# Two preln attention layers with a routed expert layer: fills rearranged, k's rotation and parts on VectorE, experts' tensors at other addresses

## What is computed

```python
x = x + attention0(layernorm(x))   # 16 heads of 16, rotary q and k, window of 128
x = x + experts(layernorm(x))      # 8 experts, the best 2 for each token, silu(a) * b
x = x + attention1(layernorm(x))   # 16 heads of 16, xpos q and k, causal, biases
x = x + ternary(x)                 # x @ quantised weight

# attention1
q_mat = split_heads(x @ Wq.T + bq)
k_mat = split_heads(x @ Wv.T + bv)
v_mat = split_heads(x @ Wk.T + bk)
q_mat, k_mat = _xpos_rotate(q_mat, k_mat)
scores = jnp.einsum('bhqd,bhkd->bhqk', q_mat, k_mat) / math.sqrt(DH * NUM_HEADS)
...
return inter @ Wo.T + bo
```

## Time and profile before

| what | us |
|---|---|
| median of three runs | 2888.07 |
| the three runs | 2873.35, 2892.66, 2888.07 |
| the profiled execution | 2870.61 |
| its span, first to last instruction | 2868.7 |
| TensorE busy | 2463.0 |
| VectorE busy | 1714.3 |
| ScalarE busy | 1350.0 |
| GpSimd busy | 923.1 |

### The profile page before, as it was taken

One profiled execution on the slowest core, in us unless ns is written; L12 is line 12 of the kernel. 1 busy time (PEld: TensorE's weight loads), 2 busy tenths in 40 slices (PEclk: granted clock), 3 DMA queues, 4 the chain that ended last, 5 costly groups with the idle time before them and its releaser, 6 DMA issues. The chain is left out here.

```text
span 2868.7 us, 50929 instructions
## 1 busy us (share of the span) xinstructions
PE 2463.0 (86%) x17722; PEld 1682.5 (59%) x17722; DVE 1714.3 (60%) x5759; ACT 1350.0 (47%) x2419; POOL 923.1 (32%) x863
## 2 busy tenths in 40 slices
PE   3788888888889849999999982799999999998997
PEld 2455555555555528898998872455555555555553
DVE  3666676766667535444444434667676677666651
ACT  2455555555555423333333321255655555555654
POOL 2434555444553220000000015344443434444300
PEclk7899999999999969999999996799999999999998
DMA  4456555666545267877777745444455444444320
GB/s 134 152 185 212 185 181 183 205 213 190 176 156 170 75 205 250 285 267 263 267 280 265 252 146 173 119 119 143 127 146 145 134 119 118 124 135 141 117 62 15
DMA packets 259617, 490.19 MB, mean 171 GB/s; under 512 B 25609, under 2 KB 191113, under 8 KB 249417
## 3 DMA queue, kind: packets, MB, share of 16 engines
q1 hardware_dynamic: 241944, 435.23, 48.3%
q0 software_dynamic: 17456, 52.19, 5.4%
HBM read 299.65 MB, written 186.52 MB: 169 GB/s over the span
## 5 line engine op out<-in xcount | busy, mean ns | idle before, releaser
L672 ACT ACTIVATE a_pr<-a_bank 128x512 f32<-128x512 f32 (+1 forms) x1152 | 638.2, 573 | 571.2 <-PE a_bank L1080 500.6
L941 DVE CUSTOM_DVE_ANT_0 a_junk<-a_bank,a_smask 128x256 bf16<-128x256 f32 (+3 forms) x1536 | 652.1, 463 | 375.2 <-PE a_bank L1177 358.1
L1177 PE MATMUL a_bank<-a_kst,a_qst 96*128 96x256 bf16 (+3 forms) x1536 | 354.5, 297 | 76.5 <-DVE a_nmax L941 26.6
L1203 PE MATMUL a_bank<-a_qst,a_kst 98*128 98x256 bf16 (+3 forms) x1536 | 345.0, 292 | 43.0 <-ACT a_pr L672 25.2
L1221 PE MATMUL a_bank<-a_pr,a_va 128*32 128x256 f32 (+3 forms) x4096 | 350.7, 418 | 28.1 <-ACT a_pr L672 25.3
L1080 PE MATMUL a_bank<-a_mask,a_identb 128*128 128x512 bf16 (+2 forms) x1152 | 351.5, 305 | 0.0
L1177 PEld LDWEIGHTS a_bank<-a_kst,a_qst 96*128 96x128 bf16 x1536 | 127.5, 99 | 268.7 <-issue 84.1
L1426 POOL DMA_DIRECT2D results_dram<-e_yt x39 | 29.3, 751 | 619.2 <-DVE e_yt L1494 601.6
L1449 ACT ACTIVATE e_sa<-e_bank,e_b 128x512 f32<-128x512 f32 (+1 forms) x156 | 101.5, 651 | 255.9 <-PE e_bank L1539 236.0
L550 POOL DMA_INDIRECT xs<-e_rn,e_row x128 | 127.1, 993 | 294.8 <-DMA a_kst<-a_parts_dram 89.0
L1203 PEld LDWEIGHTS a_bank<-a_qst,a_kst 98*128 98x128 bf16 x1536 | 134.0, 99 | 143.7 <-ACT a_pr L672 72.9
(11 more groups left out here) (214 smaller groups left out, 5352.9 us busy)
## 6 DMA issues: line engine op xcount, KB each, us to landing
a_parts_dram<-a_parts SPq DMA_DIRECT2D x224, 256.0 KB
e_under<-ws_dram SPq DMA_DIRECT2D x20, 2048.0 KB, 9.0
e_w<-ws_dram SPq DMA_DIRECT2D x19, 2048.0 KB, 9.2
a_qst<-a_parts_dram SPq DMA_DIRECT2D x96, 384.0 KB, 7.6
a_kst<-a_parts_dram SPq DMA_DIRECT2D x96, 384.0 KB, 8.7
a_parts_dram<-a_parts SPq DMA_DIRECT2D x32, 768.0 KB
e_under<-a_parts_dram SPq DMA_DIRECT2D x64, 384.0 KB, 8.3
ws_dram<-a_ws SPq DMA_DIRECT2D x24, 1024.0 KB, 7.7
```

Of the source, the lines that this page charges most:

```text
L672: nc.scalar.activation(pr[b][:, h:h + per, :], TB_[at % 2][:, 0:per * w].rearrange("p (h w) -> p h w", h=per), ACT.Exp, scale=scale).then_ ...
L941: last = nc.vector.tensor_tensor_reduce(junk[:, at % 2, j * w:(j + 1) * w], SB_[at % 2][:, j * w:(j + 1) * w], smask[:, T - w:T], scale=-1 ...
L1177: last = nc.tensor.matmul(out[:, j * w:(j + 1) * w], q[0:ROWS, hh, qb * P:(qb + 1) * P], k[0:ROWS, hh, k0:k0 + w], start=not whole or j == ...
L1203: nc.tensor.matmul(out[:, j * w:(j + 1) * w], k[0:AUG, hh, b * P:(b + 1) * P], q[0:AUG, hh, q0:q0 + w], start=(j == 0), stop=False, skip_g ...
```

## The change

- In the second stage `ident` is allocated ahead of `under`, and `under` is 48 KB instead of 32 KB a partition: it holds `w[0]` and `w[1]`. In the first attention it lends room to three of the four stacks, `qst[0]`, `kst[0]` and `qst[1]`.
- In both attentions, for batch 0 only, k's rotation and k's two differences of the split are VectorE's instead of GpSimd's.
- In the third stage GpSimd's constants stand behind the eight gathers of batch 0.
- In the third stage the statistics of batch 0 are taken tile by tile, each behind the tile's last mix.
- The bias product's due time is 0.70 instead of 0.22, behind k's parts of batch 0.
- TensorE's transposes in `turn` wait for each normalised tile by itself, in all batches.

```diff
@@ in turn(i)
-                              (1.0 + 0.015 * t, ("stats", n, t))]
+                              (1.0 + 0.015 * t if n else 0.925 + 0.022 * t, ("stats", n, t))]
...
-            out.append((0.22, ("bias",)))
+            out.append((0.70, ("bias",)))
@@ in pipeline
-            qst, kst = ([under[0:AUG, a * H * T // 2:(a + 1) * H * T // 2].bitcast(BF16)
-                         .rearrange("p (h t) -> p h t", h=H)] for a in range(2))
-            qst.append(sb("qst1", [AUG, H, T], BF16))
-            kst.append(sb("kst1", [AUG, H, T], BF16))
+            parts_of = [under[0:AUG, n * H * T // 2:(n + 1) * H * T // 2].bitcast(BF16)
+                        .rearrange("p (h t) -> p h t", h=H) for n in range(3)]
+            qst = [parts_of[0], parts_of[2]]
+            kst = [parts_of[1], sb("kst1", [AUG, H, T], BF16)]
@@ GpSimd
+            def constants():
...
+            if not mixed:
+                constants()
...
+                    if (m, k, t) == (0, 1, NT - 1):
+                        constants()
                 elif st[0] == "rope" and st[3] == 1:
...
+                    if (m, a) == (0, 1):
+                        continue
...
                 elif st[0] == "part":
...
+                    if (m, a) == (0, 1):
+                        continue
@@ VectorE, behind the products of rope
+                    if (m, a, half) == (0, 1, 1):
+                        dve.wait_ge(bank_free[1], bank_use["project", m, a] + 1)
+                        nc.vector.tensor_tensor(qk[:, a, 0, :], rt[:, 0, :], rt[:, 1, :], ALU.subtract)
+                        nc.vector.tensor_tensor(qk[:, a, 1, :], rt[:, 2, :], rt[:, 3, :], ALU.add).then_inc(qk_rotated, 1)
+                elif st[0] == "part" and st[1:3] == (0, 1):
+                    m, a, p = st[1:]
+                    if p == 0:
+                        dve.wait_ge(part0_done, a + 1)
+                        dve.wait_ge(rest1_done, a)
+                        nc.vector.tensor_tensor(qk[:, a], qk[:, a], parts[:, a, 0], ALU.subtract).then_inc(rest1_done, 1)
+                    else:
+                        dve.wait_ge(part1_done, a + 1)
+                        dve.wait_ge(part2_done, a)
+                        nc.vector.tensor_tensor(parts[:, a, 2], qk[:, a], parts[:, a, 1], ALU.subtract)\
+                            .then_inc(part2_done, 1)
@@ TensorE, turn
-                    pe.wait_ge(xn_done, NT * (m + 1))
                     pe.wait_ge(bank_free[c], bank_use["turn", m, 0])
                     for t in range(NT):
+                        pe.wait_ge(xn_done, NT * m + t + 1)
@@ in experts
-        under = sb("under", [P, H * T])
-        w = [under[:, 0:2 * NW].rearrange("p (l n) -> p l n", l=2)]
+        ident = sb("ident", [P, P])
+        under = sb("under", [P, 4 * NW])
+        w = [under[:, i * 2 * NW:(i + 1) * 2 * NW].rearrange("p (l n) -> p l n", l=2) for i in range(2)]
...
-        ident = sb("ident", [P, P])
-        w.append(sb("w1", [P, 2, NW]))
```

## The result

| | before | after |
|---|---|---|
| median, us | 2882.83 (9 runs, 2873.35 to 2892.66) | 2869.81 (9 runs, 2864.23 to 2884.29) |
| ratio | | 0.9955, interval 0.9938 to 0.9972 |
| profiled execution, us | 2870.6 | 2873.49 |

The account below looks back on a forecast made before the run. TensorE was taken to bound the experts' stage, and k's last part, stored and reloaded, each attention's fill. 3.0 + 0.65 + 1.25 + 5.7 = 10.6 us off 2888.07 gave 2877.5, range 2858 to 2895.

Parts of the forecast that it names:

- K on VectorE, first attention: First fill: k's rotation and parts on VectorE, taking turns with GpSimd, end k's last part 3.0 us earlier.
- the transposes' 0.65: First fill: TensorE's transposes waiting tile by tile start earlier, 0.65 us less; zero cost in later batches.
- SyncE is no later: First fill: q's three stores and a load, 0.7 us each, fit between 35.6 and 39.15, before k's stores.
- Second attention: Second fill: k's last part comes earlier by two terms, 1.25 us and 5.7 us.
- The first term: Second fill: of the bias product's 4 us only 1.25 arrive, because batch 1's work precedes batch 0's rotary products on VectorE.
- the second: Second fill: with k on VectorE, k's last part ends 10.25 us after q's rotation instead of 15.96, 5.7 us less.
- rival 2 or 5: Rival 2: second fill gives nothing, 2884.4 us, chance 0.15; rival 5: VectorE and GpSimd only take turns, 2886.2, chance 0.07.
- Constants, statistics, transposes: Second fill: whatever these edits give is swallowed by batch 1's work on VectorE, so they get nothing.
- The bias product's 4 us: Second fill: with the bias product out of the way, x's second low part runs about 4 us sooner.
- Addresses: Experts' stage: new addresses of activations and weights change nothing, taken as zero; bounds 11 us either way.
- Rival 4: Experts' stage: new addresses slow the matmuls, each per cent costing 6 us; up to 2910 us; chance of passing 1.8%: 0.10.
- Rival 1's cover: Second fill: quantisation and bias product just hidden, 1.4 us spare; rival 1 is the forecast, 6 to 14 less, chance 0.55.

Follow-up runs that it names:

- e6: e4 with batch 1's first mixes and second gathers behind the low parts, and the first fill's load of batch 1 behind k's stores; 2847.21 us, ratio 0.9924.
- e2: The kernel before with only the new tensor addresses, without the fills' edits; 2869.14 us, ratio 0.9967.
- e3: The changed kernel with k's rotation and differences of batch 0 back on GpSimd in both fills; 2869.58 us, ratio 0.9969.
- e12: e4 without the four small edits (constants, statistics, bias product, tile-wise transposes); 2857.48 us, ratio 0.9967.
- e4: The changed kernel with batch 1's second mixes, statistics and aggregate behind k's last part in the second attention's fill; 2854.86 us, ratio 0.9918.
- e11: The changed kernel without the four small edits (constants, statistics, bias product, tile-wise transposes); 2860.19 us, ratio 0.9972.
- e7: e6 with SyncE storing each part of q and k as soon as it is there, in later batches too; 2870.16 us, ratio 1.0001.
- e10: e7 with later batches' stores behind their last part, quantisation and bias product ahead of batch 1's second mixes, identity behind the weight buffers; 2839.73 us, ratio 0.991.
- e8: e4 with unused space in front of the experts' activations, putting them back at their old place, weights as changed; 2852.5 us, ratio 0.9945.

## Why the prediction came out right in time and half wrong in cause

- **Time.** Predicted 10.6 us less, measured 13. It is made of 6.2 to 7.4 us in the two fills instead of 10.6, and 6.4 in the experts' stage instead of zero. Two wrong terms cancel, so that the total came out this near is luck; the forecast's own cause is only half of the result.
- **K on VectorE, first attention: right up to k's last part.** It ends at 38.52 us where 38.5 was predicted (with the transposes' 0.65), and each pair of differences took turns as worked out. But only 1.9 us of 3.6 arrive at the scores. The failed step is "SyncE is no later". It counted when SyncE is free, which came out within 0.2 us, but not what the six stores cost after that: right behind the load of batch 1's x they take 5.48 us to issue instead of 4.20, and the loads of the stacks wait another 3.6 us instead of 3.0. e6 moved the load and got back 1.9.
- **Second attention: right up to k's last part as well**, though its parts are off. Predicted 6.95 us earlier (1.25 + 5.7), measured 6.4 and 6.5. The first term measured 0.37, the second 6.0. In the first, the last mix was put at 1750.0 by a landing that "no edit moves"; in the profile after, the load of batch 1's x went out 0.8 us later (22.2 instead of 21.4 us behind the experts' last matmul) and landed some 1 us later, and the gathers, mixes and products behind it too. In e2, which leaves the fills alone, it went out at 22.5, so no edit of the fills is shown to be the cause. Between k's last part and the stacks' loads 7.3 us pass instead of 6.1 (1774.27 to 1780.36 before): the 1.2 us are the six stores' slower issue, 4.64 instead of 3.45, which goes away with k on GpSimd (e3). Of 6.4 us 4.3 to 5.4 are left. The mark set for this part, less than 6 us earlier means rival 2 or 5, was hit, but neither rival was the cause.
- **Constants, statistics, transposes "get nothing" in the second fill: right as it stands.** The first low part starts 33.9 us behind the experts' last matmul, 33.65 before. The bias product's 4 us were right too, and so was what swallows them: with batch 1 out of the way (e12 against e4) the four edits give 3.9. In the changed kernel's own order the forecast let 1.25 of it through, and e11 shows 2.5 to 3.6, of which 0.9 is the collision with k's last part that the forecast didn't have.
- **Addresses: the step that failed.** The argument was that 0.34 and 0.36 occur with the same tensors at the same addresses, so address doesn't set the pace. It compared only tiles of the first buffer. The rows of the second, 0.36 in all 19 tiles, were not looked at; they would have shown half of the output tiles at the slow pace throughout, and the gain of up to 11 us as a chance of its own rather than a bound. That one condition doesn't decide alone doesn't make it worth nothing. The mark "over 3 us shorter" was hit. Rival 4's price per per cent was right (6 us; the stage got 1.0% shorter, 6.4 us), its sign wrong.
- **Rival 1's cover.** The quantisation and the bias product stayed hidden in the changed kernel, as predicted; in e7 they are in the open.

## What to carry to other kernels

When a producer gets faster, follow its product through the queue that carries it on: what else is issued there in between, how many transfers really need the last piece, and what those transfers now overtake. e7 gained 3.7 us in two fills and lost 17 in nine turns by starting stores 1 us earlier, so keep a reordering to the batch for which it is meant. And read a claim like "address doesn't matter" off all users of the address, not off the one that shows both values.

## What the runs showed of the hardware

- TensorE's pace for 128x256 outputs at full granted clock was 113.7, 117.8 or 120 ns per matmul, constant over a tile, with nothing waiting. It changed when the second weight buffer moved 10.3 KB down, with the identity and the biases, also for matmuls that read the first buffer, left exactly in its place (e10); and at the old place it depended on which of the loop's tiles it was. Moving the activations by 8 KB changed nothing (e8). The Trainium skill, "SBUF — State Buffer", section "Who interferes with whom", holds that only the port pair that VectorE and GpSimd share causes contention; for VectorE and GpSimd the rows agree (1.23 against 0.68 us in the first fill), but no such pair is at work in these matmuls, and by measurement the place of a buffer counts all the same. The mechanism is open.
- SyncE took 3.45 to 5.82 us to issue the same six stores, 0.58 to 0.97 each: the shorter its pause before them, the longer (figures in e6).
- An indirect gather landed 2.8 us after its issue in e6, and 8.7 (10.4 in another turn) in e7, where four loads of SyncE's queue went out just before it and four more within 3 us.
